# A selective-scan block on one core: drive of 12 of 24 units a chunk by TensorE in alternation, replicated rows by DMA, dt by one product, five slots for dlr and dur

## What is computed

```python
# b = 8 images, K = 4 directions, 192 channels d, 16 states n, L = 4096 positions
xz = einsum('bhwc,ec->bhwe', x, in_proj_w); xc, z = split(xz)
xa = silu(conv3x3(xc) + conv_b)                 # pre stage
xs = stack of xa read row-wise, column-wise, and both reversed
x_dbl = einsum('bkdl,kcd->bkcl', xs, x_proj_w)  # 38 rows: dts 6, Bs 16, Cs 16
delta = softplus(einsum('bkrl,kdr->bkdl', dts, dt_proj_w) + dt_proj_b)
dA = exp(delta * A)
h[t] = dA[t] * h[t-1] + (delta[t] * xs[t]) * Bs[t]   # for each d and n
y[t] = sum over n of h[t] * Cs[t]
out_y = y + xs * Ds                              # four directions are added
```

## Time and profile before

| | us |
|---|---|
| median of 3 runs (lowest, highest) | 12123.86 (12122.49, 12130.55) |
| span of the profiled execution | 12091.3 |
| of it the stretch 690 to 10205, units of the scan phase | 9515 |
| post phase, from 10205 | 1886 |

### The profile page before, as it was taken

How to read it: one execution, slowest core, us unless ns; L and a number is a source line. 1 busy time by engine, 2 the same in 40 slices (tenths; PEclk the granted TensorE clock), 3 DMA queues, 4 the chain that set the end, 5 groups by cost and what they waited for, 6 DMA issues and landing times. The chain is left out here.

```text
span 12091.3 us, 236659 instructions
## 1 busy us (share of the span) xinstructions
PE 10600.3 (88%) x92230; PEld 5356.3 (44%) x92230; DVE 10737.4 (89%) x6810; ACT 8063.5 (67%) x13314; POOL 9746.4 (81%) x4234
## 2 busy tenths in 40 slices
PE   8978888888888888888888888888888887999999
PEld 5633333333333333333333333333333333778778
DVE  7889999999999999999999999999999998555554
ACT  4367777777777777777777777777777775444443
POOL 2179999999999999999999999999999997433330
...
GB/s 106 105 126 116 126 134 120 115 130 134 121 120 131 134 120 122 127 136 121 117 127 134 116 118 127 135 118 123 127 136 119 123 126 109 66 62 44 66 61 12
DMA packets 385055, 1363.71 MB, mean 113 GB/s; under 512 B 55526, under 2 KB 56230, under 8 KB 382156
## 3 DMA queue, kind: packets, MB, share of 16 engines
...
...
## 5 line engine op out<-in xcount | busy, mean ns | idle before, releaser
L959 POOL TENSOR_TENSOR HC<-H,crep 128x1024 f32<-128x1024 f32 x3072 | 7194.8, 2371 | 407.2 <-DVE H L775 319.0
L775 DVE TENSOR_TENSOR_SCAN H<-E,car,psum 128x1024 f32<-128x1024 f32 x1920 | 4468.5, 2342 | 144.5 <-PE psum L662 90.6
L859 ACT ACTIVATE E<-dlr,am 128x1024 f32<-128x1024 f32 x2560 | 2909.4, 1145 | 38.4 <-DVE H L775 34.5
L616 PE MATMUL psum<-sx,selb 96*128 96x512 f32 x4864 | 2023.7, 509 | 837.5 <-DVE H L775 580.1
L684 PE MATMUL psum<-HC,sely 128*32 128x512 f32 x12288 | 2408.9, 666 | 29.4 <-POOL HC L959 28.3
L753 DVE TENSOR_TENSOR psum<-dur,psum 128x1024 f32<-128x1024 f32 x1792 | 2168.2, 1210 | 143.9 <-PE psum L616 137.8
L616 PEld LDWEIGHTS psum<-sx,selb 96*128 96x128 f32 x4864 | 877.0, 221 | 2930.2 <-DVE H L775 1745.1
L662 PE MATMUL psum<-diag,dluT 128*32 128x128 f32 x49152 | 1628.7, 287 | 438.8 <-DVE H L775 401.0
L662 PEld LDWEIGHTS psum<-diag,dluT 128*32 128x32 f32 x49152 | 1396.6, 116 | 993.6 <-DVE H L775 922.4
L775 DVE TENSOR_TENSOR_SCAN H<-E,psum 128x1024 f32<-128x1024 f32 x640 | 1452.2, 2283 | 40.2 <-PE psum L662 13.7
L645 PE MATMUL psum<-wx,idn 96*32 96x512 f32 x2298 | 1321.8, 681 | 0.0
...
## 6 DMA issues: line engine op xcount, KB each, us to landing
dur<-scr_dlu SPq DMA_DIRECT2D x1024, 384.0 KB, 6.4
dlr<-scr_dl SPq DMA_DIRECT2D x1024, 384.0 KB, 6.5
scr_dl<-dlt SPq DMA_DIRECT2D x256, 384.0 KB, 3.0
scr_dlu<-dlu SPq DMA_DIRECT2D x256, 384.0 KB, 8.6
scr_yk<-yt SPq DMA_DIRECT2D x256, 384.0 KB, 6.4
yp<-scr_yk SPq DMA_DIRECT2D x128, 384.0 KB, 6.6
scr_xa<-xs SPq DMA_DIRECT2D x64, 384.0 KB, 3.5
scr_sz<-xs SPq DMA_DIRECT2D x64, 384.0 KB, 3.4
```

The lines of the kernel that those rows point to most:

```text
L616: r = e.matmul(o[:, sub * 512:(sub + 1) * 512], selb[:, which, :], sx[:, c % 2, sub * 512:(sub + 1) * 512], start=True, stop=True)
L775: e.tensor_tensor_scan(H[:, un % NH, ::step], decay[:, ::step], drive[:, ::step], init, ALU.mult, ALU.add).then_inc(scan_done)
L859: e.activation(o, dlr[:, slot(m, j), :], ACT.Exp, scale=am[:, ae:ae + 1]).then_inc(exp_done)
L959: e.tensor_tensor(HC[:, un % NHC, :], H[:, un % NH, :], crep[:, g, :], ALU.mult).then_inc(hc_done)
```

## The change

`ORDER` is now one row for all steps, (2, 3, 2, 3, 2, 3, 0, 1, 0, 1, 0, 1), and both g = 3 and g = 1 are DIAGONAL. So units at odd places are DIAGONAL, those at even places DIRECT, and place 2 is POOLED: 10 DIRECT, 12 DIAGONAL, 2 POOLED a chunk. ACT makes 64 diagonals a chunk instead of 32, spread by the table `DIAGS`. `project` gives 128 rows: besides what was there, the C rows and four B rows once more in the last 32, which ACT copies to dlt and SP writes to DRAM (`out_bc`); brep and crep are then read back replicated by DMA (`in_brep`, `in_crep`), and `rep` goes, with its matmuls and ACT copies. `busy` goes too. The dt product is one fp32r matmul per 512 columns over 102 rows, in which split weights (made once on DVE at the start) meet the split rows of sx. dlr and dur have five slots and are loaded for one j at a time. delta has a second buffer, which is yt, the tile of `copy_y`. HC has six buffers instead of seven, dbu one instead of two. An exponential is issued two units ahead, and a carry copies two cells at once. `project` stands at place 4 of the even step, `delta` at 7 and 10, the split on DVE after scan 6.

```diff
-    GPOOL, GDIAG = 1, 3
+    GPOOL, GDIAG = 2, (3, 1)
+    GREP = (2, 3, 0, 1)
     DIRECT, POOLED, DIAGONAL = 0, 1, 2
-    ORDER = ((2, 0, 0, 1, 1, 3, 3, 2, 1, 0, 3, 2), (1, 3, 0, 3, 1, 3, 2, 2, 2, 0, 0, 1))
-    KIND = tuple(tuple(DIAGONAL if g == GDIAG else POOLED if g == GPOOL and x in pooled else DIRECT for x, g in enumerate(row))
-                 for row, pooled in zip(ORDER, ((3, 8), (0, 4))))
...
+    ORDER = (2, 3, 2, 3, 2, 3, 0, 1, 0, 1, 0, 1)
+    KIND = tuple(DIAGONAL if g in GDIAG else POOLED if x == 2 else DIRECT for x, g in enumerate(ORDER))
+    NDIAG = 4 * len(GDIAG)
+    DIAGS = (0, 0, 15, 3, 0, 8, 7, 0, 8, 3, 10, 0, 7, 3, 0, 0, 0, 0, 0, 0, 0, 0, 0, 0)
+    DIAG_AT = 15
+    NSLOT = 5
...
-    dlr = T("dlr", [128, 2 * NJ, TC])
-    dur = T("dur", [128, 2 * NJ, TC])
+    dlr = T("dlr", [128, NSLOT, TC])
+    dur = T("dur", [128, NSLOT, TC])
     crep = T("crep", [128, NG, TC])
     brep = T("brep", [128, TC])
-    NE, NH, NHC, NDB = 3, 4, 7, 2
+    NE, NH, NHC, NDB = 3, 4, 6, 1
...
-    dlt = T("dlt", [C + NR, TC])
-    dl, dts = dlt[0:C, :], dlt[C:C + NR, :]
+    dlt = T("dlt", [128, TC])
+    dl, bc = (dlt[0:C, :], yt[:]), dlt[C:128, :]
...
-        def spread_rows(t, name, m, landed):
+        def spread_rows(t, rows, m, j, landed):
             for q in range(4):
-                e.dma_start(t[32 * q:32 * q + 32, NJ * (m % 2):NJ * (m % 2) + NJ, :],
-                            S[name][m % 2].rearrange("(j d) t -> d j t", j=NJ)).then_inc(landed[m % 2], 16)
-
-        def in_dur(m):
+                e.dma_start(t[32 * q:32 * q + 32, slot(m, j), :],
+                            rows[32 * j:32 * j + 32, :]).then_inc(landed[slot(m, j)], 16)
+
+        def in_dur(m, j):
             e.wait_ge(dlu_out, 16 * (m + 1))
-            if m >= 2:
-                e.wait_ge(mul_done, muls(last_of(m - 2, kinds=(DIRECT,))) + 1)
-                e.wait_ge(pool_mul_done, pooled(12 * (m - 1)))
-            spread_rows(dur, "dlu", m, dur_in)
-
-        def in_dlr(m):
-            e.wait_ge(dl_out, 16 * (m + 1))
-            if m >= 2:
-                e.wait_ge(exp_done, 12 * (m - 1))
-            spread_rows(dlr, "dl", m, dlr_in)
+            if before(m, j):
+                mb, jb = before(m, j)
+                e.wait_ge(mul_done, muls(last_of(mb, j=jb, kinds=(DIRECT,))) + 1)
+                if jb == 2:
+                    e.wait_ge(pool_mul_done, mb + 1)
+            spread_rows(dur, S["dlu"][m % 2], m, j, dur_in)
+
+        def in_dlr(m, j):
+            e.wait_ge(dl_out[m % 2], 16 * (m // 2 + 1))
+            if before(m, j):
+                mb, jb = before(m, j)
+                e.wait_ge(exp_done, last_of(mb, j=jb) + 1)
+            spread_rows(dlr, S["dl"][m % 4], m, j, dlr_in)
...
+        def in_brep(c):
+            e.wait_ge(bc_out, 16 * (c + 1))
+            if c:
+                e.wait_ge(pool_mul_done, 2 * c)
+            for q in range(4):
+                e.dma_start(brep[32 * q:32 * q + 32, :], S["bc"][c % 2, NS + q, :].partition_broadcast(32)).then_inc(brep_in, 16)
+
+        def in_crep(c, i):
+            e.wait_ge(bc_out, 16 * (c + 1))
+            if c:
+                e.wait_ge(hc_done, last_of(2 * c - 1, g=GREP[2 * i + 1]) + 1)
+            g0 = GREP[2 * i]
+            for q in range(4):
+                e.dma_start(crep[32 * q:32 * q + 32, 2 * i:2 * i + 2, :],
+                            S["bc"][c % 2, 4 * g0 + q:4 * g0 + q + 5:4, :].partition_broadcast(32)).then_inc(crep_in[i], 16)
...
+            c = n // 2 + 1
+            more = n + 1 < NSTEP
             if n % 2 == 0:
+                if more:
+                    in_dlr(n + 1, 1)
+                    in_dur(n + 1, 0)
                 if n:
-                    in_dlr(n + 1)
-                if n:
-                    out_dlu(n + 1)
-                if n:
-                    in_dur(n + 1)
-                if n:
+                    in_crep(c - 1, 1)
                     store_y(n - 1)
...
+                if c < NCHUNK:
+                    out_bc(c)
+                if more:
+                    in_dlr(n + 1, 2)
+                    in_dur(n + 1, 2)
+                    in_dlr(n + 1, 0)
+                    in_dur(n + 1, 1)
+                if n + 2 < NSTEP:
+                    out_dlu(n + 2)
+                    out_dl(n + 2)
+                    out_dl(n + 3)
             else:
-                if n + 1 < NSTEP:
-                    out_dl(n + 1)
-                if n + 1 < NSTEP:
-                    in_dlr(n + 1)
-                if n:
-                    store_y(n - 1)
-                if n + 1 < NSTEP:
-                    out_dlu(n + 1)
-                if n + 1 < NSTEP:
-                    in_dur(n + 1)
+                if more:
+                    in_dlr(n + 1, 1)
+                    in_dur(n + 1, 1)
+                    in_dlr(n + 1, 0)
+                    in_dur(n + 1, 0)
+                if n + 2 < NSTEP:
+                    out_dlu(n + 2)
+                store_y(n - 1)
                 load_y(n + 1)
-                if n + 2 < NSTEP:
-                    out_dl(n + 2)
+                if more:
+                    in_dur(n + 1, 2)
+                if c < NCHUNK:
+                    in_brep(c)
+                if more:
+                    in_dlr(n + 1, 2)
+                if c < NCHUNK:
+                    in_crep(c, 0)
         store_y(NSTEP - 1)
         e.wait_ge(y_stored, 16 * NSTEP)
 
...
-                spread(P[un % 2], m // 2, 2 * g).then_inc(fill_done)
+                spread(P[un % 2], m // 2, g // 2).then_inc(fill_done)
             else:
                 e.wait_ge(lt_copied, m + 1)
-                e.wait_ge(diag_made, NBLK * 4 * (m // 2 + 1))
+                at = 4 * GDIAG.index(g)
+                e.wait_ge(diag_made, NBLK * NDIAG * (m // 2) + NBLK * (at + 4))
                 for i in range(NBLK):
                     for q in range(4):
                         r = e.matmul(P[un % 2][32 * q:32 * q + 32, i * 128:(i + 1) * 128],
-                                     dluT[:, m % 2, i, 32 * j:32 * j + 32], diag[:, i, q, :], start=True, stop=True)
+                                     dluT[:, m % 2, i, 32 * j:32 * j + 32], diag[:, i, at + q, :], start=True, stop=True)
...
             n, x = divmod(un, 12)
@@ -707,49 +745,33 @@
             if n == NSTEP:
                 continue
             if n % 2 == 0:
-                if x == 2 and n > 1:
-                    rep(c - 1, 3)
-                    busy(1)
-                    rep(c - 1, 4)
-                    busy(2)
-                if x == 6:
-                    turn_dlu(2 * (c - 1) + 1, 0)
-                if x == 7:
-                    turn_dlu(2 * (c - 1) + 1, 1)
-                if x in (7, 9):
-                    busy(1)
+                if x == 1:
+                    turn_dlu(n + 1, 0)
+                    turn_dlu(n + 1, 1)
+                if x == 4 and c < NCHUNK:
+                    project(c, 0)
+                if x == 4 and c < NCHUNK:
+                    project(c, 1)
+                if x == 7 and c < NCHUNK:
+                    delta(2 * c)
                 if x == 10 and c < NCHUNK:
-                    project(c, 0)
-                    project(c, 1)
+                    delta(2 * c + 1)
             else:
-                if x == 1 and c < NCHUNK:
-                    delta(2 * c)
-                if x == 2 and c < NCHUNK:
-                    turn_b(c)
-                if x == 3 and c < NCHUNK:
-                    rep(c, 0)
-                if x == 7 and c < NCHUNK:
+                if x == 0 and c < NCHUNK:
                     turn_dlu(2 * c, 0)
                     turn_dlu(2 * c, 1)
-                if x in (6, 7):
-                    busy(1)
-                if x == 11:
-                    busy(2)
-                if x == 8 and c < NCHUNK:
-                    delta(2 * c + 1)
-                if x == 10 and c < NCHUNK:
-                    rep(c, 1)
-                    rep(c, 2)
+                if x == 4 and c < NCHUNK:
+                    turn_b(c)
...
-            if c < NCHUNK and n % 2 == 1 and x == 0:
+            if c < NCHUNK and n % 2 == 0 and x == 6:
                 split(c)
...
@@ -796,36 +826,27 @@
             e.wait_ge(x_done, c + 1)
             if c >= 2:
                 e.wait_ge(fill_done, fills(24 * (c - 1)))
-            e.copy(dts, stage[C:C + NR, :])
-            e.copy(sx[:, c % 2, :], stage[0:C, :]).then_inc(sx_copied)
+            if c:
+                e.wait_ge(bc_out, 16 * c)
+            e.copy(bc, stage[C:128, :]).then_inc(bc_copied)
+            e.copy(sx[:, c % 2, :], stage[0:C + NR, :]).then_inc(sx_copied)
...
+        def ahead(un):
+            if un + 1 < NUNIT and kind(un + 1) == POOLED:
+                exp(un + 1)
+            if un + 2 < NUNIT and kind(un + 2) != POOLED:
+                exp(un + 2)
+
...
+            cells = car[:, c0:c1 + 1:c1 - c0] if c1 > c0 else car[:, c0:c1 - 1 if c1 else None:c1 - c0]
             e.wait_ge(scan_done, un + 1)
```

(2 more changed lines are left out.)

305 lines of the change are left out of this document (153 added, 152 removed).

## The result

| | before | changed |
|---|---|---|
| median of the runs | 12123.2 us | 11577.3 us |
| lowest to highest, 4 runs each | 12121.9 to 12130.6 | 11573.6 to 11587.0 |
| ratio, 95% interval | | 0.9552 (0.9540 to 0.9564) |
| span of the profiled execution | 12091.3 us | 11572.8 us |

The change saves 546 us (4.5%). The forecast was 11,495 us, so it was 82 us too low; the result lies within the range of 11,350 to 11,800. In the profiled executions the difference to the forecast is larger, 11572.8 against 11461, 112 us, since the median now stands only 4.5 us above the span and not 32.6. An execution's time is 1.8 us above its span, so the profiled execution of the kernel before was itself some 29 us quicker than the quickest of the four timed ones; gains between spans come out 28 us smaller (518.5 us) than the gain between medians (546).

What follows compares the result with a forecast made beforehand. DVE bounds the scan stage: 74.6 us a chunk less 4.9 of work, idle unchanged at 2.3, gives 69.7; span 12091.3 - 630 = 11461, plus 32.6 to the median, say 11,495 us. Range 11,350 to 11,800 us.

Steps and rivals of the forecast that it cites:

- DVE as the bound, four multiplies less: Scan stage: DVE, 97% busy, sets the pace; four multiplies leave, so its work falls 4.9 us a chunk, 630 us in all.
- POOL, ACT: Scan stage, per chunk: POOL's work falls from 70.5 to 65.8 us, ACT's goes from 54.7 to 58.2 us.
- no reserve for a larger gain: POOL with all its present waits would allow a 69.8 us chunk, about DVE's 69.7, so no more could be gained.
- the 3.70 us lump: PE's projection (forecast 3.60 us) in unit 4 of the even step doesn't fit: 0.45 us of stall a chunk.
- The first third of dlr: Odd step's load, queued behind two others on SP: little reserve, taken as nothing up to 0.5 us a chunk, bound 3.
- DMA late: Rival: SP's queue order fails by 2 us a chunk, scans wait for the exponential's output; about 11,750 us, chance 0.10.
- none of them is on the path: PE: the 9 filler products, dropped with five replications, are not on the path that sets the end; no cost.
- the clock term: PE at its lower clock for a fifth of 12 unit pairs: 1.6 us a chunk worked out, 1.0 us taken.
- 0.65 us a pair: At PE's lower clock a DIAGONAL and DIRECT unit pair asks 6.4 us of PE against DVE's 5.77.
- the rival: PE paces through a clock low for 40% of the scan, filler products being gone: about 11,850 us, chance 0.20.
- Replication by DMA at no cost: DMA engines: 2.6 MB more a chunk, 11.9 MB in all, take 55 us of 70 and lie beside other work.
- Start and end under 10 us: Kernel start changes by less than 10 us either way; the stage after the scan does not change.

## Why the prediction was right, and where it was off

- **DVE as the bound, four multiplies less.** Right. The group counts 1273 multiplies at 1210 ns, against 1.21 us used from the earlier trace rows; the run without the P unit prices two of them within 0.20 us of the 2.48 used. The stretch between second and last scan got 4.2 us a chunk shorter, which is 4.9 less the 0.7 us of additional idle time. A chunk of 70.3 us lies in the 69 to 70.5 forecast, idle time of 3.05 us just above the 2 to 3.
- **POOL, ACT.** Right to the tenth: 8383.9 / 127.3 = 65.9 us of POOL a chunk (65.8 forecast) and 7405.8 / 127.3 = 58.2 us of ACT (58.2). POOL's waits in the new trace are 4.5 us a chunk (4.0 taken), and DVE and POOL come out at the same length, as said. That POOL has "no reserve for a larger gain" is not shown: in the run with half of each multiply it stood at 96.8%, but DVE hardly waited for it.
The projection is the 3.70 us lump behind a G fill that was expected, and the D fill behind it makes DVE wait 126 times for 57.6 us (counted by the scan's place in the step), 0.46 us a chunk where 0.45 was forecast; the rest of the 89.1 us of D fills stands at other places. But it is not the largest piece of the idle time, as said ahead: the G fills are, with 144.1 us.
- **The first third of dlr: the term that was mis-sized.** The prediction found the place, the order of the queue and the softplus with its table loads behind it, called it the one with little reserve, and then took nothing for it, up to 0.5. It costs 117 us, 0.9 us a chunk; the bound of 3 us held. Measured from the start of scan 7, the third is issued after 4.3 us, which is 3.7 us behind the first of the three loads, and has landed after 10.7 us in the median chunk, in time for the scan due at 15.0 us; so for the usual chunk the working was right. It had one figure for all chunks, "some 8 us in the new queue". It left out that in 21 of 128 chunks yp and u are issued right ahead: there the third lands after 15.0 us, when the scan is already due. The prediction's own sign of "DMA late", scans that wait for an E held up by dlr, is in the new profile; it was the right mechanism at half its price, and it had a chance of 0.10. The forecast's idle time without this term, 2.3 us, is near what the run with the early dlr has: (110.9 + 95.7 + 7.1 + 1.1 + 0.3) / 127.2 = 1.7 us a chunk in its rows of waits, and 2.1 with the short gaps that have no such row.
- **Removing the filler products: "none of them is on the path".** Wrong. Taking them out of the old kernel costs 57 us, and four a chunk, put into the gaps of the changed one, are worth 111 us. They were off the path as work, and on it as what keeps the clock up before a long fill. The size of the clock term (1.0 us a chunk) came out about right, 144.1 / 127.3 = 1.1 us of waits for G fills, but by luck, since the working behind it did not hold: low stretches were to be spread evenly, at 0.65 us a pair. It is one place in each step, up to 3.64 us for one fill instead of 1.95. The 0.65 us also rests on a row read wrongly. The 2.63 us of the earlier trace rows is not a G fill at the lower level; the granted clock changed within it, and its mean from 5021.62 to 5024.25 us is 0.71. At 0.50 throughout it takes 3.64 us. A pair would then ask for 3.64 + 1.22 + 2.57 = 7.4 us and lose 1.7 us to DVE's 5.77, not 0.65; a fifth of the pairs spread evenly would have cost 4 us a chunk, which nothing in the new trace shows.
- **The clock would not fall as far as the rival had it.** Right: 0.96, better than 0.89 before, and better still than the 0.81 of the old kernel without its fillers. Why it rose is not isolated by a run; that a regular alternation keeps PE busy is the prediction's argument and not shown.
- **Replication by DMA at no cost.** Right: 171 GB/s as calculated (11.9 MB in 70 us), at a DMA share of 0.69 where 0.75 was forecast, and cutting nearly all of its bytes moved nothing.
- **Start and end under 10 us.** The start costs 8 us, but by a stall after the first scan, not before it; the last stage costs 6 us, for which I have no explanation.

The sum was off by 112 us of span: 14 us at the ends and 97 in the chunks, nearly all of it idle time of DVE. The late dlr by itself would account for that: without it the kernel has 2.1 us of idle time a chunk, a little under the 2.3 of the forecast. So would the missing products in PE's gaps, which weigh as much; the forecast paid for those under the name of the clock.
